# A recommendation model on one core: all four rounds of Gram matmuls, then all four rounds of top layers

## The reference

```python
x = _mlp(dense_x, bot, sigmoid_last=False)             # 13 -> 512 -> 256 -> 64
pooled = jax.vmap(lambda tab, ix: jnp.take(tab, ix, axis=0).sum(axis=1))(tables, indices)
Tcat = jnp.concatenate([x[:, None, :], jnp.transpose(pooled, (1, 0, 2))], axis=1)   # 27 vectors of 64
Z = jnp.einsum('bim,bjm->bij', Tcat, Tcat)             # their products in pairs, per sample
li, lj = jnp.tril_indices(27, k=-1)
R = jnp.concatenate([x, Z[:, li, lj]], axis=1)         # 64 + 351 = 415 features
return _mlp(R, top, sigmoid_last=True)                 # 415 -> 512 -> 256 -> 1
```

## Time and profile before

| | |
|---|---|
| median of 3 runs | 3036.29 us (3034.28 to 3039.0) |
| profiled execution | 3039.01 us, its span 3037.2 us |
| TensorE busy in the span | 2880.8 us (95%) |
| granted TensorE clock, mean | 0.968 |
| Gram matmuls (line 732) | 1024 passes, 138.9 us busy |
| diagonal copies (line 377), DVE and ACT | 128 each; 64.8 and 63.4 us busy |

### The profile page before, as it was taken

One profiled execution on the slowest core, in us unless ns is written; L12 is line 12 of the kernel. 1 busy time (PEld: TensorE's weight loads), 2 busy tenths in 40 slices (PEclk: granted clock), 3 DMA queues, 4 the chain that ended last, 5 costly groups with the idle time before them and its releaser, 6 DMA issues.

```text
span 3037.2 us, 50871 instructions
## 1 busy us (share of the span) xinstructions
PE 2880.8 (95%) x16980; PEld 1655.1 (54%) x16980; DVE 2372.7 (78%) x3358; ACT 1923.9 (63%) x2475; POOL 2037.3 (67%) x1639
## 2 busy tenths in 40 slices
PE   6999999999999999999999999999999999999798
PEld 2455555555555555555555555555555555557574
DVE  4598888888889888898888988888888888863221
ACT  3666767677676776767767667676676766762232
POOL 3277877888888888888888788888888888400000
PEclk9999999999999999999999999999999999997668
DMA  2112122121221212212122121221212212008711
GB/s 66 58 29 70 27 70 67 29 70 26 70 68 29 70 27 70 68 29 70 27 71 68 29 70 27 70 68 29 70 27 70 68 29 68 19 24 122 128 35 29
DMA packets 165642, 164.47 MB, mean 54 GB/s; under 512 B 108859, under 2 KB 127083, under 8 KB 160231
## 3 DMA queue, kind: packets, MB, share of 16 engines
q1 hardware_dynamic: 114135, 110.94, 13.0%
q0 software_dynamic: 51200, 52.53, 8.9%
q10 hardware_dynamic: 272, 0.52, 0.1%
HBM read 143.83 MB, written 20.05 MB: 54 GB/s over the span
## 4 chain that ended last, share of the span: by engine, by line
PE 75%; DVE 15%; issue 5%; ACT 3%; DMA 1%; SPq 1%; DVEq 0%; ACTq 0%; POOL 0%; POOLq 0%
PE ps L665 48%; PE ps L648 17%; PE ps L615 5%; DVE onehot_c L1027 5%; PE ps L732 4%; DVE rowmax L955 4%; DVE onehot_p L1022 2%; DVE rows L1056 1%; DVE pooled_sb L1033 1%; ACT counts L806 1%; ACT pooled_sb L797 0%; ACT parts L769 0%; ACT parts L776 0%; DVE scratch L918 0%; DVE idx_t L908 0%
## 5 line engine op out<-in xcount | busy, mean ns | idle before, releaser
L589 POOL DMA_INDIRECT rows<-in_L_rec_tables,look x1600 | 2022.5, 1264 | 550.0 <-issue 479.5
L665 PE MATMUL ps<-counts,parts 128*128 128x512 fp8e3 x8232 | 2158.9, 388 | 0.0
L806 ACT CAST counts<-ps 128x792 int32<-128x792 f32 (+1 forms) x1848 | 1509.1, 824 | 821.2 <-PE ps L648 804.0
L665 PEld LDWEIGHTS ps<-counts,parts 128*128 128x128 f16 x8232 | 779.1, 96 | 597.0 <-issue 1.6
L648 PE MATMUL ps<-onehot_c,onehot_p 120*128 120x198 bf16 x7224 | 957.2, 252 | 95.4 <-DVE onehot_c L1027 85.8
L648 PEld LDWEIGHTS ps<-onehot_c,onehot_p 120*128 120x128 bf16 x7224 | 665.9, 98 | 613.4 <-ACT counts L806 128.9
L1027 DVE TENSOR_TENSOR onehot_c<-column_c,weighted_s 120x1584 bf16<-120x1584 bf16 x924 | 901.2, 975 | 0.0
L1022 DVE TENSOR_TENSOR onehot_p<-iota_by_unit,place 120x1024 bf16<-120x1024 bf16 x924 | 636.0, 688 | 315.3 <-PE ps L648 292.8
L1056 DVE TENSOR_REDUCE rows<-rows 128x64 f32<-128x384 f32 (+1 forms) x240 | 188.5, 785 | 9.4 <-DVE pooled_sb L1033 9.4
L377 DVE COPY zt<-ps 32x208 f32<-32x208 f32 x128 | 64.8, 507 | 150.5 <-PE ps L732 148.6
L983 DVE SCALAR_TENSOR_TENSOR raw<-raw,coef_next,parts 128x896 f32<-128x896 f32 x147 | 168.1, 1144 | 0.3 <-ACT parts L769 0.3
(11 more groups left out here) (82 smaller groups left out, 537.5 us busy)
## 6 DMA issues: line engine op xcount, KB each, us to landing
raw<-in_L_rec_tables SPq DMA_DIRECT2D x21, 1792.0 KB
raw<-in_L_rec_tables SPq DMA_DIRECT2D x21, 1344.0 KB
rows<-in_L_rec_tables,look POOLq DMA_INDIRECT x1600, 2.5
pooled<-pooled_sb SPq DMA_DIRECT2D x84, 128.0 KB, 2.3
slots<-pooled SPq DMA_DIRECT2D x30, 352.0 KB, 8.0
products<-zt SPq DMA_DIRECT2D x16, 351.0 KB
idx_raw<-in_r_indices SPq DMA_DIRECT2D x21, 159.4 KB
gathered<-bags_t SPq DMA_DIRECT2D x42, 64.0 KB
```

The lines of the kernel that those rows point to most:

```text
L589: nc.gpsimd.indirect_dma_start(rows[:, s, l, :], None, rows_flat, bass.IndirectOffsetOnAxis(ap=look[:, c, s * PL + l:s * PL + l + 1].bitca ...
L665: mm = nc.tensor.matmul(acc[k % 2][:, 0:NB], parts[:, j, :], count_bytes[k % 2][:, j % COLS, 0:NB, j // COLS], start=(j == 0), stop=(j == ...
L806: nc.scalar.copy(counts[k % 2][:, :, u * UG * GS:(u * UG + g) * GS].rearrange("p c (g s) -> p g c s", s=GS), unit_ps[u % 2][:, 0:g, 0:GC]. ...
```

## The change

PE gets all four rounds of Grams first, then the wait for all 64 steps of diagonals, then the four rounds of top layers. ACT gets the same order. The wait for `top_act` inside the Grams and the waits for diagonals inside each `top_mlp` go. DVE, SP and GpSimd have the same instructions in the same order. In the changed kernel the Gram matmuls are on line 730, and ACT's activations on line 888.

```diff
--- before.py
+++ after.py
@@ -723,8 +723,6 @@
                     if b >= 4:
                         pe.wait_ge(diag_act, b - 2)
                         pe.wait_ge(diag_dve, b - 2)
-                    if r >= 2 and b == r * GRAMS_PER_TILE + 2:
-                        pe.wait_ge(top_act, TOP_STEPS * (r - 1))
                     for x in range(GRAMS):
                         g = b % GRAMS_PER_TILE // 2 * GRAMS + x
                         for half in range(2):
@@ -739,16 +737,14 @@
             def top_mlp(r):
                 pe.wait_ge(dense_in, 16 * TILES)
                 pe.wait_ge(pairs_in[r], 16 * NPIECE)
-                done = GRAMS_PER_TILE * min(r + 2, TILES)
-                pe.wait_ge(diag_act, done)
-                pe.wait_ge(diag_dve, done)
                 mlp(top_tiles, top_banks, top_mm, top_act, TOP_STEPS * r, TOP_STEPS * (r + 1))
 
-            make_grams(0)
-            for r in range(1, TILES):
+            for r in range(TILES):
                 make_grams(r)
-                top_mlp(r - 1)
-            top_mlp(TILES - 1)
+            pe.wait_ge(diag_act, NGRAM)
+            pe.wait_ge(diag_dve, NGRAM)
+            for r in range(TILES):
+                top_mlp(r)
 
 
         @block.scalar
@@ -892,11 +888,10 @@
                     nc.scalar.activation(dst, top_banks[i % 2][0:mm, :], ACT.Sigmoid if l == 2 else ACT.Relu,
                                          bias=bias).then_inc(top_act, 1)
 
-            diagonals(0)
-            for r in range(1, TILES):
+            for r in range(TILES):
                 diagonals(r)
-                top_activations(r - 1)
-            top_activations(TILES - 1)
+            for r in range(TILES):
+                top_activations(r)
 
 
         @block.vector
```

## The result

| | before | after |
|---|---|---|
| median of 6 runs | 3037.14 us (3034.28 to 3039.59) | 3015.89 us (3013.24 to 3018.84) |
| profiled execution | 3039.01 us, span 3037.2 | 3013.24 us, span 3011.4 |
| first Gram to the end of the span | 271.92 us | 248.91 us |

The ratio is 0.993, with a 95% interval of 0.9918 to 0.9943: 21.3 us less, 17 to 25 by the interval. 3013.7 was forecast, 22.6 less than the median of the three runs known then (3036.29).

The account below looks back on a forecast made before the run. TensorE was taken as the bound. 2905.87 (first layer's start) + 28.30 + 2 x 25.86 + 28.73 = 3014.62 us, 22.6 under the 3037.2 span; off the 3036.29 median that gave 3013.7 us, range 3009 to 3019.5.

Parts of the forecast that it names:

- gaps between Grams and layers: TensorE idle before layers: the 14.63 us wait for pairs and one 2.34 us wait on diagonals go, 16.97 us.
- low clock in the first layers: First layer of each round: one slow at 17.80 us instead of three, the others 15.36, saving 4.9 us.
- Gram rounds: restarts, less the wait on slots: Grams on TensorE: two restarts of 0.37 us removed, 0.7 together; wait for round 3's input taken as 0.
- rest of the layers: Layers after the first in each round: about 10.50 us a round, as before.
- the sign: First layer after the Grams: one slow one of 17.4 to 18.2 us, three others of about 15.4.
- rival of a warm start: First layer after the Grams runs at the full clock: 2.4 us less, 3011.3 us; chance 8%.
- Slots of round 3: Input loads on SP's queue for the last Grams: land at 2868.4, wanted at 2868.6, so wait 0.
- rival of late slots: Round 3's Grams wait 1 to 3.3 us for their loads on SP's queue: 3015 to 3017 us; chance 12%.
- Pairs: SP's stores and reloads into `feats` for the layers: smallest slack 40 us, in round 1, so no wait.
- rival of no gain: SP's stores and reloads of pairs set the end; would need 40 us more on each round; chance 2%.
- The slower rivals: Clock stays low in the layers: 22.4 us more a round, about 3101 us for all four; chance 2%.
- rival of a low clock in every round: Each round's first layer still starts at the low clock, 2.4 us three times: 3021 us; chance 4%.

Follow-up runs that it names:

- The experiment with three rounds first: Kernel before, with Grams of rounds 0 to 2 ahead of layers 0 and Grams of round 3 between layers 0 and 1: 3021.40 us, 0.9950 of the kernel before.
- the two traces without a gap: Changed kernel with top layers in banks 0 and 1, alone (3013.32 us) and with round 3's slots loaded before round 0's pairs are reloaded (3013.41 us).
- the kernel with free banks: Changed kernel with top layers in banks 0 and 1, so the first layer need not wait for the last diagonals: 3013.32 us, 0.9924 of the kernel before.

## Why the prediction was right, point by point

The mechanism came out as forecast: one gap in place of three, Grams in one block, one slow first layer in place of three.

**The sum, from the first Gram to the end.** 23.0 us measured in the profiles, 22.6 forecast:

| term | forecast | measured in the two traces |
|---|---|---|
| gaps between Grams and layers | 16.97 | 14.63 + 2 x 2.34 - 2.19 = 17.12 |
| low clock in the first layers | 4.9 | 68.77 - (16.96 + 3 x 15.36) = 5.73 |
| Gram rounds: restarts, less the wait on slots | 0.7 - 0 | 138.99 - 138.83 = 0.16 |
| rest of the layers | 0 | 0.00 |

(68.77 is the sum of the four first layers in the earlier trace rows. 138.99 and 138.83 are the Gram rounds: from the first Gram to the last copy, in the kernel before 69.29 + 2 x 34.85.)

The total is nearer than its terms. The clock gave back 0.8 more than forecast and the wait on slots took 0.6 that the forecast had at 0; that the two nearly cancel is luck. By medians the gain is a little smaller, 21.3, 21.8 and 22.0 us in the three comparisons.

**Gaps.** As forecast. The experiment with three rounds first shows the wait for the pairs gone while two waits on diagonals (2.29 and 2.37 us) are still there.

**The clock.** The step held: low to the end of the Grams, one slow first layer, three at 15.36. The size was off by 0.8 us. I took the mean of three first layers of the kernel before, 17.80; the three of the changed kernel have a mean of 17.18, and two of them lie under the 17.4 to 18.2 that I had given as the sign. How long the first layer stays at 0.50 differs from trace to trace: 3.2 us in the trace above and 4 in the second of the changed kernel. In the two traces without a gap it is about 2 us (16.46 and 16.48 us for the layer), less than in every trace with one (16.96 to 18.22); whether the gap makes that difference, two traces don't show.

My rival of a warm start, from the Trainium skill ("TensorE: Matmul & The Clock Gate", Part 1), by which activity releases the clock, did not come about: 138.25 us of a fully busy TensorE stayed at 0.50, as the row of the kernel with free banks shows. The trace disagrees with the rule for these passes; why they don't release the clock, no run here tells.

**Slots of round 3.** The forecast had them land at 2868.4 and wanted at 2868.6. The margin of 0.2 us was right to within a microsecond, and so small that it came out on either side. The chain of waits of the changed kernel shows the last landing just ahead of the Grams:

```profile
2863.08 3.35 DMA slots<-gathered
2866.43 0.04 issue
2866.48 8.70 PE ps L730 x61
```

The last load took 3.35 us from issue to landing, not 2.4. I chose 0 out of 0 to 3.3; it was 0.56, 0.25 and 0 us, under the 1 to 3.3 of the rival of late slots.

**Pairs.** No wait on `feats` anywhere. SP did the pairs of rounds 2 and 3 within 2 us of where the forecast had them (first Gram to first Gram), beside Grams and layers:

```profile
2884.19 7.21 SPq L508 DMA_DIRECT2D products<-zt  x4
2895.83 10.17 SPq L513 DMA_DIRECT2D feats<-products  x29
2906.10 7.30 SPq L508 DMA_DIRECT2D products<-zt  x4
2917.78 9.73 SPq L513 DMA_DIRECT2D feats<-products  x29
```

The rival of no gain needed less than I wrote. SP takes the rounds one after the other, so a delay in each adds up: by the forecast's own times round 3 has 51 us of slack and three delayed rounds ahead of its landing, so about 17 us a round would do, not 40. Nothing near that came.

**The slower rivals.** The clock rose in the first layer and stayed up through three more rounds. The rival of a low clock in every round is refuted by the same rows. What can cost the whole gain, SP's order, is named in the sum, but I didn't list it as a rival.

## What to carry to other kernels

When a transfer's answer is awaited by the next step of the same round, put the other rounds' independent work into the wait, and check first that the queue behind the transfers delivers that work's input in time: the same order on TensorE was worth 21 us or nothing. Count the work that follows a switch of kind too, since each return from Grams to layers cost a stretch at the low clock (1.1 to 2.9 us here). And compare the stage in two traces from its own first instruction: 2.8 of the 25.8 us between these spans came from ahead of it.

## What the runs showed of the hardware

The Gram passes (fp32, 64 x 128 weights, 104 columns) keep their pace at either clock. In the kernel with three rounds first, the Grams of round 3 start at the full clock, behind layers. The clock falls to 0.50 within 4 us of their start at 2899.98, with TensorE busy throughout (busy time of PE, granted clock):

```profile
2903.00:2903.50 0.50, 0.50 (x6) 1.00 0.07 12
2903.50:2904.00 0.50, 0.50 (x8) 0.59 0.16 37
```

So it takes no gap for the clock to fall either. VectorE's first copy at the start of the stage, where the clock is 0.50, and its first copy in round 3:

```profile
2770.61 2.08 DVE L377 COPY zt<-ps 32x208 f32<-32x208 f32 x4 [5.28 <-PE ps L732]
...
2904.65 2.09 DVE L377 COPY zt<-ps 32x208 f32<-32x208 f32 x4 [32.81 <-PE ps L732]
```

From the first Gram (2765.96 and 2899.98) to that copy it is 4.65 us at 0.50 and 4.67 us with the first 3.5 at 1.00, while a layer's pass goes from 0.86 to 0.43 us. So the low clock costs nothing in this stage until layers follow.
